# Delta-rule attention and mixture of experts on one core: a 128-column ones operand, output weights fetched per head, and the inverse of D⁻¹+M with its transpose turned by TensorE

## The reference

```python
q = scale ** 2 * _rmsn(q, EPS_QK)      # q, k, v: projection, causal convolution of 4 taps, silu
k = scale * _rmsn(k, EPS_QK)
def step(S, inputs):
    q_t, k_t, v_t, g_t, b_t = inputs
    S = S * jnp.exp(g_t)[..., None]                # a decay per channel
    kv = jnp.einsum('bhd,bhdv->bhv', k_t, S)
    delta = b_t[..., None] * (v_t - kv)
    S = S + k_t[..., None] * delta[:, :, None, :]
    o = jnp.einsum('bhd,bhdv->bhv', q_t, S)
    return (S, o)
...
out = _rmsn(out, EPS_NORM) * o_norm_w * jax.nn.sigmoid(gate)
return out.reshape(B, T, H * D) @ Wo.T
```

## Time and profile before

| | us |
|---|---|
| median of three runs | 6977.61 |
| lowest, highest | 6950.22, 7022.47 |
| the profiled execution: its span | 6987.9 |
| PE matmul busy | 6382.5 (91%) |
| DVE busy | 4977.7 (71%) |
| ACT busy | 3034.5 (43%) |
| POOL busy | 1945.3 (28%) |

### The profile page before, as it was taken

How to read it: one execution, slowest core, us unless ns; L and a number is a source line. 1 busy time by engine, 2 the same in 40 slices (tenths; PEclk the granted TensorE clock), 3 DMA queues, 4 the chain that set the end, 5 groups by cost and what they waited for, 6 DMA issues and landing times.

```text
span 6987.9 us, 133956 instructions
## 1 busy us (share of the span) xinstructions
PE 6382.5 (91%) x40960; PEld 5321.9 (76%) x40960; DVE 4977.7 (71%) x13890; ACT 3034.5 (43%) x5936; POOL 1945.3 (28%) x2752
## 2 busy tenths in 40 slices
PE   7999999989999989999999989999999999989999
PEld 5877787778777777778777877778787877865555
DVE  5777776777777777777777777777777777745555
ACT  3444444444444444444444444444444544411111
POOL 3323333323233233333233323333333332300000
PEclk8999999999999999999999999999999999999999
DMA  2000000000000000000000000000000000000000
GB/s 72 13 10 13 13 10 14 13 10 13 10 13 13 10 13 13 13 11 13 10 13 13 13 10 13 11 13 13 14 10 14 13 14 10 7 27 10 12 9 12
DMA packets 36993, 97.47 MB, mean 14 GB/s; under 512 B 3057, under 2 KB 19697, under 8 KB 36081
## 3 DMA queue, kind: packets, MB, share of 16 engines
q1 hardware_dynamic: 36336, 89.68, 4.0%
HBM read 81.28 MB, written 8.39 MB: 13 GB/s over the span
## 4 chain that ended last, share of the span: by engine, by line
PE 61%; DVE 26%; issue 9%; ACT 2%; DVEq 1%; POOL 0%; ACTq 0%; POOLq 0%
PE bank L890 10%; PE bank L1066 7%; PE bank L907 7%; PE bank L920 7%; DVE kq L584 6%; PE bank L1022 5%; PE bank L917 5%; PE bank L1038 5%; DVE lx L567 4%; DVE AT L594 4%; PE bank L873 3%; PE bank L1076 3%; DVE yv L628 3%; DVE yq L628 3%; PE bank L996 2%
## 5 line engine op out<-in xcount | busy, mean ns | idle before, releaser
L293 POOL TENSOR_TENSOR kl<-kl,tot 128x256 f32<-128x256 f32 x768 | 527.7, 687 | 2206.8 <-PE bank L890 2206.6
L890 PE MATMUL bank<-kq,kl 128*128 128x128 f32 x6144 | 893.0, 290 | 260.8 <-DVE AT L594 260.6
L567 DVE SCALAR_TENSOR_TENSOR lx<-bank,sc,mask 128x64 f32<-128x64 f32 x3584 | 770.6, 276 | 500.4 <-PE bank L890 425.8
L890 PEld LDWEIGHTS bank<-kq,kl 128*128 128x128 f32 x6144 | 787.2, 200 | 297.1 <-issue 278.3
L907 PE MATMUL bank<-T,lx 128*128 128x128 f32 x6144 | 867.6, 287 | 93.5 <-DVE T L615 88.6
L907 PEld LDWEIGHTS bank<-T,lx 128*128 128x128 f32 x6144 | 791.7, 201 | 111.4 <-DVE T L615 105.7
L920 PE MATMUL bank<-TT,lx 128*128 128x64 f32 x6144 | 839.8, 281 | 1.0 <-ACT lx L390 1.0
L584 DVE TENSOR_TENSOR kq<-kq,tot 128x256 f32<-128x256 f32 x1536 | 814.6, 571 | 0.0
L390 ACT ACTIVATE lx<-bank 128x256 f32<-128x256 f32 x768 | 296.4, 386 | 1139.5 <-PE bank L907 1139.5
L917 PEld LDWEIGHTS bank<-lx,TT 128*128 128x128 f32 x5120 | 631.6, 191 | 207.6 <-ACT lx L390 146.9
L873 PE MATMUL bank<-xT,par 128*128 128x512 f32 x1536 | 772.1, 599 | 0.8 <-ACT gaT L369 0.8
(11 more groups left out here) (161 smaller groups left out, 12478.1 us busy)
## 6 DMA issues: line engine op xcount, KB each, us to landing
par<-params_dram SPq DMA_DIRECT2D x128, 519.0 KB, 3.5
xall<-x_dram SPq DMA_DIRECT2D x16, 512.0 KB, 3.8
out_dram<-xall SPq DMA_DIRECT2D x16, 512.0 KB, 2.9
lx<-ffn_dram SPq DMA_DIRECT2D x1, 3456.0 KB, 11.1
wo_sb<-wo_dram SPq DMA_DIRECT2D x1, 1024.0 KB, 5.1
wfa_sb<-wfa_dram SPq DMA_DIRECT2D x1, 128.0 KB, 2.3
wga_sb<-wga_dram SPq DMA_DIRECT2D x1, 128.0 KB, 2.1
wb_sb<-wb_dram SPq DMA_DIRECT2D x1, 8.0 KB, 2.9
```

What stands on the lines that cost most here:

```text
L293: pool.tensor_tensor(halves(kl[:, :], h)[:, :, 0, :], src, totr.broadcast_to([P, SEQ // (2 * h), h]), ALU.mult).then_inc(s["kl_ready"], 1)
L567: ins = dve.scalar_tensor_tensor(out=halves(chunk(LT[l], n), h)[:, :, 1, :], in0=b_lvl[:, n * HALF:(n + 1) * HALF].rearrange("p (m h) -> p ...
L890: ins = pe.matmul(dst[:, :, n], chunk(left, n), right[:, :, n, :, 1, :], start=True, stop=True)
```

## The change

1. `ones` has 128 columns in place of one, and each of the 12 products of the row sums moves 128 columns. They overlap in the bank; the first column of each, the only one read, is right, since a later product lands to the right of it.
2. T and TT are now those of (D⁻¹ + M)⁻¹ = TD. They start as diag(sc), made by POOL with a multiplication in place of a copy. `LT` needs no scale but at level 0, so `l_evict` is one instruction of 256 columns. `w_evict` has no scale either.
3. `lt_times_t` makes only the 64 columns that are used. The products for TT at levels 1 to 5 (L917 in the lines of before) are gone, and DVE's subtractions from TT at levels 0 to 5. Instead PE turns the new T after levels 0 to 5 (`turn_t`) and ACT copies half of the columns to TT (`tt_evict`). `XS` is packed and has one buffer; a padded `XW` serves the last level.
4. The first update of T is four instructions with the scalar `nsc` = -sc; `nsc` is one more small instruction.
5. Output weights come per head, 128 KB each, in two buffers (`load_wo` on SP's queue); `o_norm_w` is applied by ACT when it copies `ogT`.

```diff
-        ones = sb("ones", [P, 1])
+        ones = sb("ones", [P, P])
@@ SP
+            def load_wo(m, p, h):
+
+                if not isinstance(m, int) or m >= 2:
+                    sp.wait_ge(s["out_mm"], 2 * (m - 1))
+                    sp.sem_inc(s["sp_go"], 1)
+                sp.dma_start(wo_h[p][:, :], wo[h]).then_inc(wo_in[p], 16)
@@ POOL
-                    pool.tensor_copy(T[:, :], ident4[:, :]).then_inc(s["t_init"], 1)
+                    pool.tensor_tensor(T[:, :].rearrange("p (n c) -> p n c", c=P), eye, diag, ALU.mult
+                                       ).then_inc(s["t_init"], 1)
...
@@ ACT
+                def tt_evict(l):
+                    h = 1 << l
+                    act.wait_ge(s["turn_mm"], (LEVELS - 1) * iB + l + 1)
+                    if l == 0:
+                        act.wait_ge(s["tt_init"], iB + 1)
+                    act.activation(halves(TT[pB][:, :], h)[:, :, 1, :], halves(b_y[:, :], h)[:, :, 1, :], ACT.Copy
+                                   ).then_inc(s["tt_ev"], 1)
...
                     if slot == 5 and A:
                         if B:
+                            tt_evict(3)
                             x_evict(4)
...
@@ DVE, l_evict
+                    if l:
+                        dve.tensor_tensor(halves(LT[l], h)[:, :, 1, :],
+                                          b_lvl[:, 0:256].rearrange("p (m h) -> p m h", h=h),
+                                          mask[l][:, :].rearrange("p (m h) -> p m h", h=h), ALU.mult
+                                          ).then_inc(s["lt_done"], 1)
+                        return
@@ PE
-                        ins = pe.matmul(chunk(b_x, n), chunk(LT[l], n), chunk(T, n), start=True, stop=True)
+                        ins = pe.matmul(b_x[:, n * HALF:(n + 1) * HALF].rearrange("p (m h) -> p m h", h=h),
+                                        chunk(LT[l], n), halves(chunk(T, n), h)[:, :, 0, :], start=True, stop=True)
+                def turn_t(l):
+
+                    pe.wait_ge(s["t_upd"], (LEVELS - 1) * iB + l + 1)
+                    if l == 0:
+                        after(pe, s["tt_upd"], iB)
+                    else:
+                        pe.wait_ge(s["tt_ev"], (LEVELS - 1) * iB + l)
+                    for n in range(NCH):
+                        ins = pe.transpose(chunk(b_y, n), chunk(T, n), ident)
+                    ins.then_inc(s["turn_mm"], 1)
...
+                    if B and slot >= 2:
+                        turn_t(slot - 2)
                     if B and slot >= 1:
                         lt_times_t(slot - 1)
...
-                                ins = pe.matmul(b_v[:, NCH * t + n:NCH * t + n + 1], chunk(y3[t], n), ones[:, 0:1],
+                                at = NCH * t + n
+                                ins = pe.matmul(b_v[:, at:at + P], chunk(y3[t], n), ones[:, :],
                                                 start=True, stop=True)
```

More of the change, by code:

```diff
@@ L76, in delta_moe @@
         par = [sb(f"par{p}", [P, PAR]) for p in range(2)]
-        wo_sb = sb("wo_sb", [P, HEADS * HID])
+        wo_h = [sb(f"wo{p}", [P, HID]) for p in range(2)]
         onw_sb = sb("onw_sb", [P, 1])
@@ L114, in delta_moe @@
         sc = [sb(f"sc{p}", [P, NCH]) for p in range(2)]
+        nsc = [sb(f"nsc{p}", [P, NCH]) for p in range(2)]
         rinv = [sb(f"rinv{p}", [P, NCH]) for p in range(2)]
@@ L121, in delta_moe @@
         LT = [lx[:, l * SEQ:(l + 1) * SEQ] for l in range(LEVELS)]
-        XS = [lx[:, (LEVELS + l) * SEQ:(LEVELS + l + 1) * SEQ] for l in range(LEVELS)]
+        XS = lx[:, LEVELS * SEQ:LEVELS * SEQ + SEQ // 2]
+        XW = lx[:, (LEVELS + 1) * SEQ:(LEVELS + 2) * SEQ]
         T = sb("T", [P, SEQ])
@@ L195, in _ @@
         def _(sp):
-            for src, dst in ((wfa, wfa_sb), (wga, wga_sb), (wb, wb_sb), (wo, wo_sb), (onw, onw_sb), (gate_w, gw_sb)):
+            for src, dst in ((wfa, wfa_sb), (wga, wga_sb), (wb, wb_sb), (onw, onw_sb), (gate_w, gw_sb)):
                 sp.dma_start(dst[:, :], src).then_inc(s["w_in"], 16)
@@ L442, in step @@
                         after(act, s["out_mm"], 2 * iC)
-                        act.activation(ogT[:, :], b_k[:, :], ACT.Copy).then_inc(s["ogt_ev"], 1)
+                        act.activation(ogT[:, :], b_k[:, :], ACT.Copy, scale=onw_sb[:, 0:1]).then_inc(s["ogt_ev"], 1)
                     if B and slot >= 2 and not (A and slot in (5, 6)):
+                        tt_evict(slot - 2)
                         x_evict(slot - 1)
@@ L847, in batch_stage @@
                 after(pe, s["qk_ev"], LEVELS * (HEADS * bn - 1))
-                after(pe, s["tt_upd"], LEVELS * (HEADS * bn - 1))
+                after(pe, s["tt_upd"], HEADS * bn - 1)
                 turn_x((b_lvl, b_y), "xnT_mm")
@@ L1038, in step @@
                                 ins = pe.matmul(bank[half][:, n * HID:(n + 1) * HID], chunk(ogT, 2 * half + n),
-                                                wo_sb[:, bass.ds(hc * HID, HID)], start=True, stop=True)
+                                                wo_h[p][:, :], start=True, stop=True)
                             ins.then_inc(s["out_mm"], 1)
@@ L1134 @@
         "wb_dram": down_first(A["Wb"]).reshape(P, KT * HEADS),
-        "wo_dram": A["Wo"].reshape(HID, HEADS, P).transpose(2, 1, 0).reshape(P, HEADS * HID),
+        "wo_dram": A["Wo"].reshape(HID, HEADS, P).transpose(1, 2, 0),
         "onw_dram": A["o_norm_w"].reshape(P, 1),
```

109 lines of the change are left out of this document (68 added, 41 removed).

## The result

| us | before | changed |
|---|---|---|
| median | 6984.91 (4 runs) | 6597.44 (4 runs) |
| lowest, highest | 6950.22, 7022.47 | 6595.44, 6598.89 |
| profiled execution: its span | 6987.9 | 6595.6 |

The ratio is 0.9445, with a 95% interval of 0.9405 to 0.9485: 387 us less. The forecast was 6640, with a range of 6430 to 6870.

A forecast was written before the change was run, and what follows sets the result against it. DVE sets the pace in slots 0 to 4, ACT in 5 to 7, PE and its clock from the sums on. Terms sum to -2.7 us a head, 127 times, -343: 6640 us, range 6560 to 6720, wider 6430 to 6870.

The forecast's parts named there:

- Sums, and their width (0): Row sums: 24 records of 128 columns cost the same as one-column records, 0 us a head (bounds 0 and 0.5).
- Slot 0 (+0.5): POOL's multiplications into T and TT delay DVE's `kq` pair and so `level(1)`: +0.5 us a head.
- Slot 1 (0): First update of T becomes four instructions, but `l_evict(1)` gains what it loses: 0 us a head.
- Slot 2 (-1.2): PE loses eight 64-column records and gains four transposes, which fill the wait for the state: -1.2 us a head.
- Slots 3 and 4 (-1.0, 0 to -1.8): DVE drops work, its `kq` pair avoids POOL, `level(5)` stops waiting; PE waits for T instead: -1.0 us a head.
- The rival that had the pair still colliding: Slot 4's `kq` pair still meets POOL, clock falls in slot 6 or 7: -0.9 us a head, 6874; chance 0.16.
- Slots 5 to 7 (+0.5): Four transposes ahead of ACT's list and a copy to TT, partly filling a pause: +0.5 us a head.
- Clock behind the sums (-1.5): Slot 7 to 0: without one-column records PE's clock no longer falls after the sums: -1.5 us a head.
- Other clock terms (-0.7 and +0.7): Old half-clock stretches, mostly at the `level(5)` wait, go: -0.7; new falls in slots 6 and 7, half of heads: +0.7.
- The rival in which the clock stays low: PE at 1.2 GHz for all of slots 4 to 7: +5 us a head, about 7650; chance 0.06.
- the rival of 6480: No clock fall in slots 6 and 7, slot 4's collision and wait entirely gone: -4.0 us a head; chance 0.20.

The follow-up runs named there:

- Taking the collision away: Changed kernel with POOL's multiplications into T and TT ahead of its first `kl_update`, and AT's diagonal made by ACT instead of DVE: 6429.01 us.
- The two runs on `l_evict`: Changed kernel with the masked copy into LT in four instructions a level again: scalar a constant, 6556.67 us; scalar read from a tile, 6771.88 us.
- the changed kernel without the stall: Changed kernel with 64 one-column memsets to an unused tile at the start of DVE's program, moving all later DVE code: 6513.59 us.

## Why the prediction was right, and where it was not

**Sums, and their width (0).** Right. 24 records of 128 columns take 2.78 us from the first start to the next work (3035.01 to 3037.79), 0.116 each; all 35 records take 0.10 us more than those of one column did. The table of the Trainium skill (TensorE: Matmul & The Clock Gate, "Back-to-back issue gap"), which the page gives for a single matmul in isolation, would by estimate have made it 94 us longer; it does not describe these records.

**Slot 0 (+0.5).** Right in cause and size: `level(1)` waits 1.12 where it waited 0.69 (medians), +0.43. The whole piece grew by 0.35 in the median; the wide operand alone had shortened it by 0.08. That the mean came out at +0.45 is luck: the stall below makes 0.39 of it. Taking the collision away gave 85 us, 0.67 a head.

**Slot 1 (0).** +0.18 in the mean, from heads behind the stalls, whose clock falls; the window 3048.0 to 3052.5 has a granted clock of 0.63:

```profile
3048.00:3052.50 4.50, 4.48 (x20) 4.02 (x21) 1.54 (x5) 0.00 (x0) 0.74 (x1) 0.63 0.00 0
```

**Slot 2 (-1.2).** -1.04 in the median. The sum as written, 0.84 + 0.44 - 0.44, is 0.84; the 1.2 comes out if the whole wait of 0.77 goes, 0.84 + 0.77 - 0.44 = 1.17. Of that wait 0.23 us stayed.

**Slots 3 and 4 (-1.0, 0 to -1.8).** -1.11 in the mean, and what I named late next was late next: PE waits 0.61 us for T ahead of the transposes (forecast 0.8), then `level(5)` follows without a wait. The two runs on `l_evict` show that this hung on 0.24 us. The rival that had the pair still colliding had a real mechanism, one DVE instruction form away. What the forecast did not see is that a meeting has no fixed loser: before, POOL's instruction started 0.05 us behind the pair in every head, and the pair was held up in 92 of 128.

**Slots 5 to 7 (+0.5).** +0.37 in the median. ACT's list from the decay to the end of the second square:

```profile
3026.41 0.71 ACT L467 ACTIVATE a<-e_sb,amp 128x512 f32<-128x512 f32 x1
...
3034.34 0.62 ACT L516 ACTIVATE yk<-k 128x512 f32<-128x512 f32 x1
```

From 3026.41 to 3034.96 are 8.55 us, against 8.45 in the earlier trace rows.

**Clock behind the sums (-1.5).** -1.27 in the mean, -1.45 in the median. The kernel with one column again, +1.69, shows the cause.

**Other clock terms (-0.7 and +0.7).** The second of them failed. The old stretches at half clock went: from level 5 to the sums the mean fell by 0.32 while the median rose by 0.37, so the slow heads gave 0.69. The new ones in slots 6 and 7 came in 17 heads, not in half of them: 52 falls of the clock are left of 162, and they take 239 us in place of 706. What was mis-sized is the waits. I gave about 1 us for ACT and 1 us for T; PE waits 0.28 and, in 97 of 127 heads, at most 0.61, and in none of these does the clock fall. In the other 30, two of each sequence, the wait for T is 0.88 to 1.39 us, and there it falls in 17. So where the wait was of the size that I named, about half of the heads lost the clock. Slots 2 to 5 and slots 5 to 7 of a head with the short waits, then slot 7 of one with the long:

```profile
3007.50:3024.00 16.50, 15.59 (x115) 13.41 (x115) 13.60 (x30) 7.83 (x15) 2.91 (x4) 1.00 0.00 0
3024.00:3036.00 12.00, 10.54 (x85) 9.43 (x84) 6.19 (x18) 11.68 (x29) 7.20 (x13) 1.00 0.15 46
2803.00:2813.00 10.00, 8.90 (x61) 8.22 (x61) 6.72 (x23) 8.15 (x16) 4.67 (x11) 0.83 0.17 56
```

```profile
2808.89 1.10 PE L969 MATMUL bank<-ident,T 128*128 128x128 f32 x4 [0.90 <-DVE T L660]
```

The rival in which the clock stays low did not come: the clock is 1.00 in slots 2 to 7 of most heads, with the transposes among the products. Whether a transpose counts for the clock as a product does, which the Trainium skill (TensorE: Matmul & The Clock Gate, "Part 4: PE-mode transpose") denies, no run here settles: none has transposes alone, and the run with products in their place changed the waits as well.

**Missing: DVE's fetch at the loop's jump back.** I costed edits by the work they hold and never by where they leave the code. The stall was there before (a wait of `level(1)` of 2.45 us in every eighth head); the change made it 4.0, and with it the changed kernel is 84 us from what its own work allows. It is most of the distance to the rival of 6480, which so had the better size for what the edits do: 6514 without the stall. In the changed kernel without the stall, levels 0 to 2 take 0.08 us a head less than before (mean), and 0.63 more with it.

**The number.** That 6640 came within 43 us of 6597 is in part luck. From level 5 to the sums the forecast was 0.8 us a head too slow. Slot 2 and the clock behind the sums were each 0.2 too good, and slot 1, where the stall shows, 0.2 as well; these errors stand against the first.

## What to carry to other kernels

Where long SBUF instructions of DVE and POOL start within half a microsecond of each other, as these did, count what a shift of 0.2 us would do in both directions; and count heads, since of two that meet either can lose. Where an engine idles on "issue" at one head in eight, look at the transfers of instructions in that window, and move the code before you tune anything else by tens of microseconds. Up to 128 columns were free here for a record that takes 0.11 us anyway, and one that moves a single column can cost the clock of all that follows.

## What the runs showed of the hardware

- Four DVE instructions on 64 columns with a scalar read per partition take 0.85 us, with a constant 0.61.
- A DVE instruction with one SBUF tile as input and one as output (the scaled identity into `AT`) is also held up by POOL: 2.33 us for four in place of 0.87.
- DVE waited up to 4.0 us (2.48 and 1.55) at the inner loop's jump back while three packets of instructions came in; 64 instructions more ahead of it took this to nothing. At the outer loop's it waited 3.3 to 4.4 us even so.
- A DVE pair with POOL's instruction starting 0.24 us behind it was held up in 110 of 128 heads (1.82 us) and free in 18 (0.75), when POOL's took 1.64 in place of 1.30; with 0.48 us it was free in all.
- A float32 transpose of 128 columns is one record and takes 0.11 us from start to start at full clock, half of the same thing written as a product.
